# RWKV block and gated FFN on one core: the first normalisation split between two engines, the first weight loads held back, a small matrix group moved

## The reference

```python
x = x + attn(layernorm(x))        # attn has its own LN first, so norm1 is a norm of a norm
x = x + ffn(layernorm(x))

# attn: h = LN(x)*g + b; hh = h shifted by one token
k, v, r = ((h*m + hh*(1-m)) @ W.T for m, W in ((mk, Wk), (mv, Wv), (mr, Wr)))
x = x + (sigmoid(r) * wkv(k, v)) @ Wo.T
h = LN(x)*g2 + b2                  # again a token shift
x = x + sigmoid(mix(h) @ Wcr.T) * (silu(mix(h) @ Wkey.T) @ Wval.T)
# ffn: silu(h @ Wgate.T) * (h @ Wup.T) @ Wdown.T
```

## Time and profile before

| | us |
|---|---|
| median of 3 runs | 1042.37 (1040.67 to 1045.35) |
| the profiled execution's own time | 1042.62 |
| its span, first to last instruction | 1040.8 |
| PE busy | 1030.8 (99%) |
| DVE / POOL / ACT busy | 746.1 / 664.5 / 538.9 |

### The profile page before, as it was taken

The page is one execution under the profiler, slowest core; times in us unless marked ns, Lnnn a source line. Parts: engine busy times, 40 slices in busy tenths (PEclk is TensorE's granted clock), DMA queues, the critical chain, the costliest instruction groups (busy, mean ns, idle before and its releaser), DMA issues.

```text
span 1040.8 us, 13820 instructions
## 1 busy us (share of the span) xinstructions
PE 1030.8 (99%) x4607; PEld 850.6 (82%) x4607; DVE 746.1 (72%) x1240; ACT 538.9 (52%) x902; POOL 664.5 (64%) x541
## 2 busy tenths in 40 slices
PE   8999999999999999999999999999999999999998
PEld 6777888888888888878888888888888888888887
DVE  7899866786576687586568577788689466666655
ACT  7866888857444445355354534333435344444442
POOL 7796673726676875777747565678683456665652
PEclk9999999999999999999999999999999999999999
DMA  9100325367867787989924565964945455445432
GB/s 349 59 21 0 60 66 118 102 204 266 329 219 292 266 277 245 353 310 313 284 99 164 196 227 172 239 236 142 298 164 196 152 169 177 149 153 162 160 103 81
DMA packets 98854, 197.09 MB, mean 189 GB/s; under 512 B 40160, under 2 KB 53344, under 8 KB 93920
## 3 DMA queue, kind: packets, MB, share of 16 engines
q1 hardware_dynamic: 74880, 146.84, 41.3%
q0 software_dynamic: 15168, 48.24, 15.1%
q10 hardware_dynamic: 8736, 1.14, 1.2%
HBM read 117.00 MB, written 74.99 MB: 184 GB/s over the span
## 4 chain that ended last, share of the span: by engine, by line
PE 86%; DVE 5%; POOL 5%; ACT 2%; issue 2%; DMA 0%; SPq 0%; ACTq 0%; DVEq 0%; POOLq 0%
PE bank L941 14%; PE bank L943 14%; PE bank L942 14%; PE bank L930 10%; PE bank L931 10%; PE bank L932 10%; POOL operand L2605 3%; PE bank L1121 2%; PE bank L1122 2%; PE bank L1123 2%; PE bank L1143 2%; PE bank L1141 2%; PE bank L1142 2%; POOL weights L2593 1%; PE bank L1005 1%
## 5 line engine op out<-in xcount | busy, mean ns | idle before, releaser
L941 PE MATMUL bank<-combo,left 128*128 128x512 f32 x672 | 262.2, 390 | 0.4 <-ACT made L1571 0.2
L943 PE MATMUL bank<-combo,left 128*128 128x512 f32 x672 | 261.5, 389 | 0.0
L942 PE MATMUL bank<-combo,left 128*128 128x512 f32 x672 | 261.5, 389 | 0.0
L2640 POOL TENSOR_TENSOR left<-quart,left 128x512 fp32r<-128x512 f32 x96 | 115.9, 1230 | 74.5 <-ACT left L1447 43.4
L941 PEld LDWEIGHTS bank<-combo,left 128*128 128x128 f32 x672 | 126.1, 188 | 28.6 <-ACT bank L1685 0.8
L943 PEld LDWEIGHTS bank<-combo,left 128*128 128x128 f32 x672 | 126.1, 188 | 26.4
L942 PEld LDWEIGHTS bank<-combo,left 128*128 128x128 f32 x672 | 126.1, 188 | 25.9
L2679 POOL TENSOR_TENSOR inner<-made,inner 128x512 fp32r<-128x512 f32 x64 | 86.1, 1368 | 61.6 <-ACT inner L1562 61.5
L2117 DVE TENSOR_TENSOR resid<-bank,resid 128x512 f32<-128x512 f32 x120 | 80.9, 686 | 51.5 <-PE bank L932 50.6
L2605 POOL TENSOR_TENSOR operand<-made,operand 128x512 fp32r<-128x512 f32 x64 | 83.2, 1353 | 34.2 <-ACT operand L1324 34.2
L930 PE MATMUL bank<-right,inner 128*128 128x512 f32 x256 | 99.6, 389 | 0.0
(11 more groups left out here) (232 smaller groups left out, 2364.9 us busy)
## 6 DMA issues: line engine op xcount, KB each, us to landing
kept_left<-left SPq DMA_DIRECT2D x24, 1792.0 KB, 8.6
left<-kept_left POOLq DMA_DIRECT2D x24, 1024.0 KB, 8.1
left<-kept_left POOLq DMA_DIRECT2D x24, 768.0 KB, 4.9
val_w<-kept_w SPq DMA_DIRECT2D x25, 512.0 KB, 5.7
quart<-wide SPq DMA_DIRECT2D x24, 512.0 KB, 3.8
tall_staged<-tall SPq DMA_DIRECT2D x32, 256.0 KB, 4.8
raw<-kept SPq DMA_DIRECT2D x32, 256.0 KB, 8.5
kept_w<-right SPq DMA_DIRECT2D x26, 256.0 KB, 7.1
```

The source lines that it names most:

```text
L941: pe.matmul(acc[:], hi, combo[:, c, k, 0, :], start=fresh and k == 0, stop=False, skip_group_check=True)
L942: pe.matmul(acc[:], hi, combo[:, c, k, 1, :], start=False, stop=False, skip_group_check=True)
L943: mm = pe.matmul(acc[:], lo, combo[:, c, k, 0, :], start=False, stop=k == 1, skip_group_check=True)
L2640: lo = pool.tensor_tensor(left[u % 2][:, 1, a[0]:a[0] + n, :], quart[:, a[0] + 1:a[0] + 1 + n, :], left[u % 2][:, 0, a[0]:a[0] + n, :].bit ...
```

## The change

ACT scales tiles 0 and 1 of block 0, with a bias (minus the mean times the scale) that DVE makes in one small instruction each; DVE scales tiles 2 and 3. ACT does this ahead of all weight tiles, makes the high parts of only two Wr tiles before the mixing of r, and the other two within it (`first_mix`). DVE makes the low part of the fourth Wr tile after it has mixed r. POOL's fifth power moves behind the low parts of r. SP waits for the second tile of `x` before it issues the weights. PE runs 15 and 18 idle transposes in place of 19 and 20, and turns block 3 at the start of unit 18.

```diff
@@ semaphores
-        first_var, first_rstd = sem("first_var"), sem("first_rstd")
+        first_var, first_rstd, first_z = sem("first_var"), sem("first_rstd"), half_set
@@ SP
             for n in range(SUBS):
                 sp.dma_start(resid[:, 0, n], x_blocks[0][:, n, :]).then_inc(x_first[n], 16)
+            sp.wait_ge(x_first[1], 16)
             load(range(ITEM_R, ITEM_O))
@@ PE, first_norm1
-                    pe.wait_ge(z1_ready, s + 1)
+                    if s < 2:
+                        pe.wait_ge(first_z, 1 + s + 1)
+                    else:
+                        pe.wait_ge(z1_ready, 1 if s == 2 else SUBS)
@@ PE, unit
+                if u == KEYS + 2:
+                    turn_value(PAIRS + 1)
                 left_there(0)
...
                 product(Z, u, A22, T4, False).then_inc(p4, 1)
                 values(5)
-                if u == KEYS + 1:
-                    turn_value(PAIRS + 1)
@@ PE, start
-            keep_running(19)
+            keep_running(15)
             first_norm1()
-            keep_running(20)
+            keep_running(18)
@@ ACT, new
+            def first_norm1():
+                for s in range(2):
+                    act.wait_ge(first_rstd, s + 1)
+                    act.wait_ge(first_var, 3 + 2 * s)
+                    act.activation(resid[:, 0, s, :], resid[:, 0, s, :], ACT.Identity, bias=offset1[:, 0, s:s + 1],
+                                   scale=rstd1[:, 0, 1, s:s + 1]).then_inc(first_z, 1)
+            def first_mix():
+                rest_of("r", 0, 0)
+                rest_of("r", 0, 1)
+                place_free("r", 0)
+                operand_hi("r", 0, 0)
+                rest_of("r", 0, 2)
+                operand_hi("r", 0, 1)
+                matrix_hi(ITEM_R, range(2, 3))
+                rest_of("r", 0, 3)
+                operand_hi("r", 0, 2)
+                matrix_hi(ITEM_R, range(3, KT))
+                operand_hi("r", 0, 3)
+                matrix_hi(ITEM_K, range(1))
@@ ACT, start
-            matrix_hi(ITEM_R)
+            first_norm1()
+            matrix_hi(ITEM_R, range(2))
             act.wait_ge(const_done, 3)
-            mixed("r", 0, behind=1, amid=lambda: matrix_hi(ITEM_K, range(1)))
+            first_mix()
@@ DVE, first_norm1 (order of the steps)
+                summed(0)
+                summed(1)
+                varied(0)
+                summed(2)
+                varied(1)
+                offset(0)
+                varied(2)
+                summed(3)
+                offset(1)
+                varied(3)
+                normed(2, 1)
+                shares(slice(0, 3), 0)
+                normed(3, SUBS - 1)
                 dve.tensor_scalar(var_eps[:, 0], stats1[:, 0, :, 1], EPS, None, ALU.add).then_inc(first_var, 1)
-                shares(slice(0, 3), 0)
@@ DVE, start
             first_norm1()
-            last_of_r_lo()
             dve.wait_ge(const_done, 7)
             mix("r", 0)
+            last_of_r_lo()
@@ POOL, start
             matrix_lo(ITEM_R, range(KT - 1))
             operand_lo("r", 0)
+            first_norm0()
             operand_lo("k", 0)
```

More of the change, by code:

```diff
@@ L1857, in first_norm1, with offset, normed @@
             def first_norm1():
-                def normed(s):
+                def offset(s):
                     dve.wait_ge(first_rstd, s + 1)
-                    norm1_tile(0, s)
+                    dve.scalar_tensor_tensor(out=offset1[:, 0, s:s + 1], in0=stats1[:, 0, s, 0:1], scalar=-1.0,
+                                             in1=rstd1[:, 0, 1, s:s + 1], op0=ALU.mult,
+                                             op1=ALU.mult).then_inc(first_var, 1)
+                def normed(s, done):
+                    dve.wait_ge(first_rstd, s + 1)
+                    dve.tensor_scalar(resid[:, 0, s, :], resid[:, 0, s, :], stats1[:, 0, s, 0:1],
+                                      rstd1[:, 0, 1, s:s + 1], ALU.subtract, ALU.mult).then_inc(z1_ready, done)
                 def summed(s):
@@ L2608, in first_norm1, with first_norm0 @@
             def first_norm1():
-                for s in range(SUBS):
-                    pool.wait_ge(first_var, s + 1)
+                for s, done in enumerate((1, 2, 4, 6)):
+                    pool.wait_ge(first_var, done)
                     pool.tensor_tensor(rstd1[:, 0, 1, s:s + 1], var_eps[:, 1, s:s + 1], minus_half[:, 1, s:s + 1],
                                        ALU.pow).then_inc(first_rstd, 1)
-                pool.wait_ge(first_var, SUBS + 1)
+            def first_norm0():
+                pool.wait_ge(first_var, 7)
                 pool.tensor_tensor(rstd1[:, 0, 0], var_eps[:, 0], minus_half[:, 0], ALU.pow).then_inc(first_rstd, 1)
```

## The result

The changed kernel took 1044.45 us (median of 22 runs, 1042.66 to 1048.43) against 1042.73 for the kernel before, measured with it (22 runs, 1040.67 to 1045.35): ratio 1.0019, 95% interval 1.0013 to 1.0026. It is slower by 1.7 us. That is inside the 0.5% that the prediction called "same", yet 22 runs a side resolve it. The forecast of 1043.3 had the sign and half of the size. The profiled execution's own time is 1044.46, its span 1042.7; that of before was 1042.62 and 1040.8.

What follows compares the result with a forecast made beforehand. Up to 106 us a chain through POOL was taken to bound the kernel, after that PE. Late at 106 us 1.0, unit 18 -0.1: +0.9 on the median 1042.37 gave 1043.3 us, range 1041.0 to 1045.0.

Steps and rivals of the forecast that it cites:

- Scaling on two engines: Block 0 start: last scaling ends at 9.25 to 9.3; first matmul moves from 13.02 to 12.3, 0.7 us won.
- The 0.65: Block 0 start: the last scaled tile is ready 0.65 us earlier than before.
- The late path at k: POOL's low parts of k start 1.3 us later, 22.3 instead of 21.03, bounds 1.05 to 1.5.
- I add 0.2, between nothing and one further long one: POOL's four low parts of r, 5.9 us before, take 0.2 longer beside DVE's low parts; a further long one is 0.45.
- The third Wr tile's place: ACT makes its high part later, so POOL starts that tile at 13.9 instead of 13.6, its 1.24 us lead waited away.
- The weights held back: SP's wait for tile 1: first weights land at 7.55, or 9.55 at worst; taken as hidden by ACT's two scalings.
- Units 17 and 18: Block 3 turned at unit 18 saves 0.1 to 0.2 us of ACT's delay; bounds -0.5 and +0.3.
- Takes back a part: POOL's idle 0.2 before 34.68 leaves it 1.0 to 1.1 us late at the power for block 1; 1.0 at 106 us.
- Rivals 1 and 2: First: the start's gain comes through, 1041.6, chance 0.22. Second: PE's stops and chain slack swallow it, 1042.3, chance 0.22.
- Rival 3: Weights land late, at 9.55; PE starts at 13.4 and POOL is some 1.1 us later still: 1044.4, chance 0.07.
- Rival 4: PE's higher clock comes late or is lost, 512-column matmuls cost 0.43 instead of 0.227 us; 1045 not excluded, chance 0.04.

Runs made afterwards that it cites:

- power moved: Kernel before with one edit: POOL's fifth power moved between the low parts of r and those of k; 1043.56 against 1042.98 us, ratio 1.0004.
- low part moved: Kernel before with one edit: DVE makes the fourth Wr tile's low part behind the mixing of r; 1043.78 against 1042.53 us, ratio 1.0011.
- the power back: Changed kernel with POOL's fifth power back ahead of its low parts; 1044.59 against 1042.89 us, ratio 1.0015.
- the candidate: Changed kernel, third Wr tile rounded before mixing, fifth power before low parts, no weight hold, POOL waiting for DVE's three small instructions; 1042.91 against 1042.53 us.
- block 3 in unit 17: Changed kernel with block 3 turned in unit 17 again, behind its sixth product; 1044.49 against 1042.89 us, ratio 1.0017.
- third Wr tile first: Changed kernel with ACT rounding three Wr tiles, not two, ahead of the mixing of r; 1043.38 against 1042.89 us, ratio 1.0005.
- small ones by: Kernel before with a POOL wait letting DVE's three small instructions go ahead of POOL's low parts; 1042.23 against 1042.98 us, ratio 0.9992.
- its repetition: Kernel before with the same POOL wait for DVE's three small instructions, run once more unchanged; 1042.40 against 1042.53 us, ratio 0.9999.

## Why the prediction was right, and where it wasn't

The time fell within the stated range, and the forecast's cause, POOL late at k, is what the trace shows. The size was half of what came: +0.9 against +1.7 us.

**Scaling on two engines: right, but credited too much.** The last scaling ran from 8.71 to 9.26; 9.25 to 9.3 was forecast. The 0.65 was worked out against a before in which the fourth tile was late. In the four executions with the usual landing the first matmul, after the later begin is taken out, comes at 12.52, 12.37 (power moved), 12.54 and, with slow transposes and the low part moved, 13.16; that of after at 12.20. The gain at the start is 0.2 to 0.3 us, not 0.7.

**The late path at k: right about POOL, on a wrong base.** K began at 22.55 for a forecast of 22.3. But before usually begins it at 20.52 to 20.55 (20.55 and 20.78, less 0.03 and 0.23 of a later begin), not at 21.03. The loss is 1.9 us instead of 1.3. It adds up from POOL's rows: the third Wr tile ends 0.7 later, one of the four low parts of r takes 1.74 in place of 1.29, the power costs 1.0, and the wait of 0.2 at k is gone. The base is off by 0.5 of this: the sum was made against one execution whose start had a bad draw. Whether such a draw reaches the end isn't shown: that execution's own time, 1042.62, is no longer than the median of 1042.73.

**"I add 0.2, between nothing and one further long one": the term that was too small.** It was one whole further long one: the four low parts of r took 6.39 for 5.9, the bound the prediction gave. I also costed the fourth Wr tile's low part, moved behind the mixing of r, only as contention for POOL. It stands ahead of the low parts of Wk and of the mixing of k on DVE's own list too. The prediction had ACT's high part of k0 ready at about 21.4; it was ready at 21.90 (21.27 and 0.63), behind DVE's mixing at 20.38 instead of 18.57. In the changed kernel that path had 0.65 us to spare, as POOL came to k at 22.55; it decides as soon as POOL is earlier, as with the power back (k at 22.12, 0.43 won and no resolved time). By itself on the kernel before, the edit cost 1.1 to 1.8 us at 27 and 1.25 in the median, where the power alone cost 0.56 and 0.58; in the candidate, which keeps it, late at 27 is 0.22 in all. So the two are parallel paths to the same point, and I never worked the second through DVE's list; but its price is not one number.

**The third Wr tile's place: right.** POOL waited for it until 13.96. Rounded earlier, it gave 1.0 us at k and brought the median from 1.72 to 0.49 over before's, the largest single repair.

**The weights held back: right where it was tested.** With and without the hold the changed kernel is equally late. It isn't free in general: with four Wr tiles wanted ahead of the mixing, ACT waited 0.96 us for the fourth. ACT's timeline after the change shows its first two roundings with no wait for a transfer ahead of them:
```profile
8.21 1.14 ACT L1323 ACTIVATE weights<-landed 128x512 fp32r<-128x512 f32 x2
```
The first weight tile was issued at 4.54 and landed 2.7 us after its issue, at 7.2. The Trainium skill (DMA: Bandwidth & Descriptors, Anatomy of one DMA), by whose fit the prediction estimated 2.6 us and a landing at 7.3, agrees for this one; the second took 3.0, the third and fourth 4.2 to 4.4.

**Units 17 and 18: not there.** The forecast -0.1 isn't resolved in the times; the run that undoes it is level with the changed kernel. In the profiles PE's distance to before changes by 0.03 from 560 to 700 us after the change, and by 0.01 with the move undone.

**"Takes back a part", 0.2 to 0.3, ahead of 106 us: it took back almost nothing.** The power for block 1 stood at 38.90, 1.48 later than in the earlier trace rows, and the matmul of 105.81 at 107.33, 1.52 later, where 1.0 was forecast. In this execution the chain had no slack. It isn't so in each: with block 3 in unit 17, which has the same start, PE was 1.40 late at 27 and 0.88 at 105.81.

**The rivals.** Rivals 1 and 2 are out: the interval lies wholly above no change. Rival 3 has about the right time (1044.4) by a wrong mechanism: in the changed kernel ACT didn't wait for weights at the start. Rival 4 isn't seen in the 512-column matmuls. The granted clock reads 1.00 from 4 us on in both kernels, also over the transposes that took 0.21 us each, so that column doesn't bear out the reading of those as half speed. The stretch after the change, PE alone:
```profile
4.00:7.50 3.50, 3.37 (x16) 1.00 0.83 298
```
The transposes of x began at 0.21 us each in five of the executions: the first 12 of 16 in "third Wr tile first" (3.17 us for all), the first 8 in "low part moved" (2.69 against 2.03), four to six in three others; in the rest they ran at 0.11 from the start. What makes them slow stays open. They cost: with 12 of them at 0.21 the first matmul came at 13.01, in the candidate, whose ACT works in the same order there, at 12.50.

**Open.** Where the 0.9 to 2.0 us that are won between 60 and 107 us go isn't settled. Between 430 and 510 us PE stops for transfers, for ACT or for POOL by up to 1.1 us, at changing places from one execution to the next; in the profile of "small ones by" a stop of 1.04 us at 483 gave back most of the gain, in its repetition none did. That the median loses it there is likely, but not shown, and nor is what sets those stops: no run here changes anything in that stretch.

## What to carry to other kernels

When an instruction is moved out of the way of one chain, cost it in its new place on its own engine's list first, with all that stands behind it, and then as contention; a 0.69 us instruction that sat in a gap became one of 1.43 in the changed kernel, 1.69 alone and 0.85 in the candidate, by where it met the other engine's list. Before you credit a gain at the start, ask whether the trace's own arrival times are usual: if an engine waits for a DMA there, the row is a draw, and a second profile is worth more than a second decimal. Pair the instructions of two profiles from the end: it shows at once in which stretches a lead is won or lost. And look for tiny instructions with absurd durations: here one showed a lockout, and one wait on the other engine removed it, though no resolved time came of it.

## What the runs showed of the hardware

A VectorE instruction of 128x4 with two SBUF inputs took 4.92 us while GpSimd ran four 128x512 subtractions back to back, and 0.15 us when GpSimd let it go first; in the run with the power back it took 1.19 us, with two copies of 1.3 us behind it. There it began 0.15 us after the first of the four, in the kernel before 0.14 after, so what decides between the two isn't shown. A 128x512 subtraction with two SBUF inputs on VectorE took 0.68 or 0.69 us with none of GpSimd's subtractions running when it began, and 0.74 to 1.81 when one was: it ended 0.58 to 0.60 us after GpSimd's next had begun, in ten executions of ten. GpSimd's next one then took 1.71 to 1.76 instead of 1.29. Of two executions of one program, the same matmul at about 104 us stood 0.8 us apart.
